# The shared network of the last batch split around the expert loop, in a gated cross-attention and mixture-of-experts block

## The reference

```python
def _L0_xattn_ref(teacher_logits, teacher_features, Wq, bq, Wk, bk):
    query = einsum('bnc,dc->bnd', teacher_features, Wq) + bq
    key = einsum('bnc,dc->bnd', teacher_features, Wk) + bk
    attention = softmax(einsum('bnd,bmd->bnm', query, key), axis=-1)
    return einsum('bln,bmn->blm', teacher_logits, attention)

def _L0_ffn_ref(x, router_w, shared_gate, shared_up, shared_down, w_gate, w_up, w_down):
    flat = x.reshape(-1, 512)
    shared_out = sigmoid(flat @ shared_gate.T) * (flat @ shared_up.T) @ shared_down.T
    weights = softmax(flat @ router_w.T, axis=-1)
    top_w, top_idx = top_k(weights, 2)
    ...
    he = sigmoid(ge) * ue                      # ge, ue, de in bfloat16, for the chosen experts
    routed = (comb[:, :, None] * de).sum(axis=1)
    return x + shared_out + routed

x = x + tanh(g_xattn[0]) * _L0_xattn_ref(_layernorm(x), ctx_1024, ...)
x = x + tanh(g_ffn[0]) * _L0_ffn_ref(_layernorm(x), ...)
```

## Time and profile before

| | us |
|---|---|
| median of three runs (lowest, highest) | 337.62 (336.86, 339.15) |
| span of the profiled execution | 339.6 |
| TensorE busy | 298.9 (88%) |
| VectorE busy | 211.9 (62%) |
| GpSimd busy | 156.9 (46%) |
| ScalarE busy | 136.3 (40%) |
| chain that ended last: PE / DMA / POOL / DVE / issue | 67 / 9 / 6 / 6 / 6% |

### The profile page before, as it was taken

How to read it: one execution, slowest core, us unless ns; L and a number is a source line. 1 busy time by engine, 2 the same in 40 slices (tenths; PEclk the granted TensorE clock), 3 DMA queues, 4 the chain that set the end, 5 groups by cost and what they waited for, 6 DMA issues and landing times.

```text
span 339.6 us, 6123 instructions
## 1 busy us (share of the span) xinstructions
PE 298.9 (88%) x1587; PEld 211.6 (62%) x1599; DVE 211.9 (62%) x580; ACT 136.3 (40%) x239; POOL 156.9 (46%) x237
## 2 busy tenths in 40 slices
PE   2678968999999999999999999699999999998280
PEld 1245845878687786878787787566666666664020
DVE  0147676748874667848357388647767677675191
ACT  1467166740667803657601562033343433333000
POOL 3041978166740384900687117115555656566100
PEclk9959977999999999999999999989999999999587
DMA  4999399512143021000029998224333333429498
GB/s 110 340 294 259 108 198 182 206 49 79 62 130 120 0 80 47 0 2 2 31 94 164 209 207 195 83 74 124 102 120 101 116 97 121 124 79 322 121 312 342
DMA packets 31444, 45.91 MB, mean 135 GB/s; under 512 B 3456, under 2 KB 21120, under 8 KB 31424
## 3 DMA queue, kind: packets, MB, share of 16 engines
q1 hardware_dynamic: 20992, 27.67, 26.7%
q0 software_dynamic: 10432, 17.99, 22.5%
HBM read 39.58 MB, written 14.72 MB: 160 GB/s over the span
## 4 chain that ended last, share of the span: by engine, by line
PE 67%; DMA 9%; POOL 6%; DVE 6%; issue 6%; ACT 2%; SPq 1%; POOLq 0%; ACTq 0%; DVEq 0%
PE bank L675 13%; PE bank L472 11%; PE bank L473 11%; PE bank L474 11%; PE bank L692 7%; POOL xg L398 4%; PE bank L467 4%; DMA acc<-x 4%; PE bank L483 3%; PE bank L667 3%; PE bank L683 2%; DMA z<-ysb,desti 2%; DMA zb<-z 2%; DVE acc L1264 1%; DVE probT_lo L983 1%
## 5 line engine op out<-in xcount | busy, mean ns | idle before, releaser
L888 ACT ACTIVATE sigc<-bank 128x352 f32<-128x352 f32 x39 | 18.1, 463 | 68.1 <-PE bank L675 68.1
L472 PE MATMUL bank<-lnT_hi,sgu_lo 128*128 128x512 f32 (+2 forms) x96 | 39.7, 414 | 1.6 <-DVE lnT_lo L983 1.6
L451 POOL DMA_INDIRECT z<-ysb,desti x36 | 36.1, 1002 | 9.7 <-issue 9.4
L473 PE MATMUL bank<-lnT_lo,sgu_hi 128*128 128x512 f32 (+2 forms) x96 | 38.5, 401 | 0.0
L474 PE MATMUL bank<-lnT_hi,sgu_hi 128*128 128x512 f32 (+2 forms) x96 | 38.4, 400 | 0.0
L675 PE MATMUL bank<-wgu_lo,xTb 128*128 x156 | 36.7, 317 | 0.0
L675 PE MATMUL bank<-wgu_hi,xTb 128*128 x156 | 36.7, 317 | 0.0
L398 POOL DMA_INDIRECT xg<-lnb,slot x32 | 31.9, 996 | 9.9 <-issue 7.3
L1231 DVE TENSOR_TENSOR hrow<-sigc,bank 128x352 bf16<-128x352 f32 x39 | 20.3, 521 | 25.2 <-ACT sigc L888 21.8
L387 POOL TENSOR_TENSOR hT_lo<-sig,hT_hi 128x512 fp32r<-128x512 f32 (+1 forms) x9 | 11.6, 1290 | 47.6 <-ACT hT_hi L798 47.5
L1237 DVE TENSOR_SCALAR ysb<-bank,wt 128x512 bf16<-128x512 f32 x39 | 29.2, 748 | 5.1 <-DMA z<-ysb,desti 2.6
(11 more groups left out here) (174 smaller groups left out, 650.1 us busy)
## 6 DMA issues: line engine op xcount, KB each, us to landing
xt<-xg SPq DMA_DIRECT2D x39, 129.0 KB, 2.1
xT_raw<-xT SPq DMA_DIRECT2D x4, 1024.0 KB, 7.8
acc<-x SPq DMA_DIRECT2D x4, 1024.0 KB, 10.0
out<-acc SPq DMA_DIRECT2D x16, 256.0 KB, 3.4
wgu_lo<-wguT POOLq DMA_DIRECT2D x2, 1408.0 KB, 14.0
wgu_hi<-wguT POOLq DMA_DIRECT2D x2, 1408.0 KB, 13.5
cx<-ctxT SPq DMA_DIRECT2D x4, 512.0 KB, 5.3
wd_sb<-wdT POOLq DMA_DIRECT2D x2, 1024.0 KB, 18.3
```

The lines of the kernel that those rows point to most:

```text
L451: nc.gpsimd.indirect_dma_start(out=z, out_offset=bass.IndirectOffsetOnAxis(ap=desti[:, r:r + 1], axis=0), in_=ysb[:, r, :], in_offset=None ...
L472: pe.matmul(dst, a_lo, b_hi, start=first, stop=False)
L473: pe.matmul(dst, a_hi, b_lo, start=False, stop=False)
L888: act.activation(sigc[:, v, :], bank[2 * v][:, 0:I], ACT.Sigmoid).then_inc(s["csig"], 1)
```

## The change

Three things change, and the order of five engines with them.

1. Of batch 3's shared network only the first piece (c = 0, which holds the logits) is done ahead of the loop; its pieces 1 and 2 and all its `down` rows come behind it. Since the loop uses what lay under them, batch 3's normalised and turned rows go to `probT_hi` and `probT_lo` (`lnT(b)`), and the tiles of the loop and of the tables lie elsewhere.
2. Batch 3's attention is pulled forward: its projections and energies are woven into batch 2's mix, its mix comes ahead of batch 2's pieces 1 and 2, which stand behind it with batch 2's `down` rows last. GpSimd's list is reordered to fit, and `wgu_hi` and `wd_sb` are issued between other pieces of it.
3. The two results of z are no longer added on TensorE. VectorE adds `za` to `acc` for tiles 0 to 5 and `zb` for all 16, GpSimd adds `za` for tiles 6 to 15. `zb` has room for all 16 tiles and comes in eight DMAs.

```diff
+        def gate_bank(b, c):
+            return bank[0 if c == 1 or (b == last_b and c == 0) else 2]
+        def up_bank(b, c):
+            return bank[1 if c == 1 or (b == last_b - 1 and c == 2) else 3]
+        def lnT(b):
+            return (probT_hi, probT_lo) if b == last_b else (lnT_hi, lnT_lo)
...
 @block.sync
-            for t in range(TT):
-                if t >= ZS:
-                    store(t - ZS)
-                sp.dma_start(zb[:, t % ZS], zt[1, :, t]).then_inc(s_zl[t % ZS], 16)
+            for i in range(0, TT, 2):
+                sp.dma_start(zb[:, i:i + 2], zt[1, :, i:i + 2]).then_inc(s_zb[i // 2], 16)
+            for t in range(TT):
+                if t < LT * last_b:
+                    sp.wait_ge(s["comb"], t + 1)
+                else:
+                    sp.wait_ge(s["shared"], t + 1)
+                sp.dma_start(out[t * P:(t + 1) * P, :], acc[:, t, :]).then_inc(s["outd"], 16)
 @block.gpsimd
+            b = last_b - 1
+            factors2(b)
+            factor1(last_b)
+            x_low(last_b)
+            rows_copy(b)
+            pool.wait_ge(s["eng"], TT)
+            pool.wait_ge(s["xTlo"], NB)
+            for k in range(KP, NT):
+                pool.dma_start(wgu_hi[:, k - KP], wguT[:, k * P:(k + 1) * P, :].rearrange("e p i -> p e i")).then_inc(s["wgu2_in"], 16)
+            scatter(b, 0)
+            factors2(last_b)
+            pool.wait_ge(s["xmm"], TT)
+            for k in range(IT):
+                pool.dma_start(wd_sb[0:KI[k], k], wdT[:, k * P:k * P + KI[k], :].rearrange("e p n -> p e n")).then_inc(s["wd_in"], 16)
+            scatter(b, 1)
+            rows_copy(last_b)
+            scatter(last_b, 0)
+            scatter(last_b, 1)
...
+            for t in range(EARLY_Z, TT):
+                pool.wait_ge(s_za[t // LT], 16)
+                nc.gpsimd.tensor_tensor(acc[:, t, :], acc[:, t, :], za[:, t, :], ALU.add).then_inc(s["z1"], 1)
 @block.tensor
+            b = last_b - 1
+            project(last_b, 0)
+            project(last_b, 1)
+            mix(b, range(0, 1))
+            energy(last_b, 0)
+            energy(last_b, 1)
+            mix(b, range(1, 2))
+            energy(last_b, 2)
+            mix(b, range(2, 3))
+            energy(last_b, 3)
+            mix(b, range(3, 4))
+            down(b - 1, 0)
+            turn_prob(last_b, 0)
+            turn_prob(last_b, 1)
+            down(b - 1, 1)
+            turn_ln2(b, 0)
+            turn_ln2(b, 1)
+            down(b - 1, 2)
+            turn_ln2(b, 2)
+            turn_ln2(b, 3)
+            down(b - 1, 3)
+            wide_shared(b, 0, 1)
+            turn_prob(last_b, 2)
+            turn_prob(last_b, 3)
+            wide_shared(b, 0, 0, range(0, 2))
+            turn_logits(b)
+            wide_shared(b, 0, 0, range(2, NT))
+            mix(last_b, range(0, 2))
+            rank(b)
+            mix(last_b, range(2, LT))
+            wide_shared(b, 1, 0)
+            wide_shared(b, 1, 1, range(0, 2))
+            turn_ln2(last_b, 0)
+            turn_ln2(last_b, 1)
+            wide_shared(b, 1, 1, range(2, NT))
+            turn_ln2(last_b, 2)
+            turn_ln2(last_b, 3)
+            wide_shared(b, 2, 0)
+            wide_shared(last_b, 0, 1)
+            wide_shared(b, 2, 1, range(0, 2))
+            turn_logits(last_b)
+            wide_shared(b, 2, 1, range(2, NT))
+            wide_shared(last_b, 0, 0)
+            rank(last_b)
+            for j in range(LT):
+                down(b, j)
...
-            for t in range(TT):
-                pe.wait_ge(s_zl[t % ZS], 16 * (t // ZS + 1))
-                at_least(pe, s["comb"], t - 3)
-                pe.matmul(bank[t % 4][:, :], identb[:], za[:, t, :], start=True, stop=False)
-                pe.matmul(bank[t % 4][:, :], identb[:], zb[:, t % ZS, :], start=False, stop=True).then_inc(s["zsum"], 1)
+            for c in range(1, IT):
+                wide_shared(last_b, c, 0)
+                wide_shared(last_b, c, 1)
+            for parts in (range(IT - 1), range(IT - 1, IT)):
+                for j in range(2):
+                    down(last_b, j, parts)
+            for j in range(2, LT):
+                down(last_b, j)
 @block.vector
+            choose(b)
+            weights(b)
+            residual(last_b, range(0, 2))
+            places(b)
+            shared_hidden(b, 0)
+            hidden_low(b, 0)
+            residual(last_b, range(2, LT))
+            ln2_apply(last_b)
...
+            choose(last_b)
+            shared_hidden(b, 2)
+            hidden_low(b, 2)
+            weights(last_b)
+            places(last_b)
...
+            for t in range(EARLY_Z):
+                add_first(t)
+            shared_hidden(last_b, 1)
+            for r in range(SLOTS):
+                dve.wait_ge(s_yd[r], 16 * len(range(r, NE, SLOTS)))
+            hidden_low(last_b, 1)
+            for t in range(0, 4):
+                add_second(t)
+            shared_hidden(last_b, 2)
+            hidden_low(last_b, 2)
+            for t in range(4, TT):
+                add_second(t)
+            for j in range(LT):
+                shared_out(last_b, j)
```

More of the change, by code:

```diff
@@ L421, in _ @@
                 nc.gpsimd.tensor_copy(lnb_rows[0], lnr2[:]).then_inc(s["rowsb"], 1)
+            for b in range(last_b - 1):
+                factors2(b)
+                if b:
+                    factor1(b + 1)
+                rows_copy(b)
                 if b == 0:
@@ L502, in turn_prob, with mix @@
                 turn(prob[:, j], j).then_inc(s["tp"], 1)
-            def mix(b):
+            def mix(b, rows=range(LT)):
                 pe.wait_ge(s["probTlo"], LT * (b + 1))
                 pe.wait_ge(s["xTlo"], b + 1)
-                for j in range(LT):
+                for j in rows:
                     if j >= 2:
                         pe.wait_ge(s["x1"], LT * b + j - 1)
+                    elif b == last_b:
+                        pe.wait_ge(s["shared"], LT * (b - 2) + j + 3)
                     elif b:
@@ L556, in wide_shared @@
                 else:
-                    pe.wait_ge(s[free], IT * b + 1)
-                o_ = half_ * I + row * P
-                for k in range(NT):
-                    if c == 0 and half_ == 0 and k == NT // 2:
-                        turn_logits(b)
-                    mm = three(bank[pair + half_][0:m, :], sgu_hi[:, k, o_:o_ + m], sgu_lo[:, k, o_:o_ + m],
-                               lnT_hi[:, k, :], lnT_lo[:, k, :], k == 0, k == NT - 1)
-                mm.then_inc(s[done], 1)
+                    pe.wait_ge(s["hid"], IT * b + 1)
@@ L598, in _ @@
             turn_prob(0, 3)
-            for b in range(NB):
-                more = b < last_b
+            for b in range(last_b - 1):
                 mix(b)
@@ L874, in _ @@
                 add_ln2(b, 3)
-                if more:
-                    prob_high(b + 1, 0)
-                    prob_high(b + 1, 1)
+                prob_high(b + 1, 0)
+                prob_high(b + 1, 1)
                 hidden_high(b, 1)
                 gate_shared(b, 2)
-                if more:
-                    prob_high(b + 1, 2)
-                    prob_high(b + 1, 3)
+                prob_high(b + 1, 2)
+                prob_high(b + 1, 3)
                 hidden_high(b, 2)
+            b = last_b - 1
+            qk(last_b)
+            act.activation(warm[:], less_mean[:], ACT.Exp)
+            for j in range(LT):
+                soft(last_b, j)
+            for j in range(LT):
+                normalise(last_b, j)
+            prob_high(last_b, 0)
+            prob_high(last_b, 1)
+            x_high(last_b)
+            for j in range(LT):
+                ln2_high(b, j)
+            rows_again(b)
+            logits_out(b)
+            prob_high(last_b, 2)
+            prob_high(last_b, 3)
+            choice_exp(b)
+            gate_shared(b, 0)
+            for j in range(LT):
+                add_ln2(b, j)
+            hidden_high(b, 0)
+            gate_shared(b, 1)
+            ln2_high(last_b, 0)
+            ln2_high(last_b, 1)
+            hidden_high(b, 1)
+            ln2_high(last_b, 2)
+            ln2_high(last_b, 3)
+            gate_shared(b, 2)
+            rows_again(last_b)
+            logits_out(last_b)
+            act.activation(warm[:], less_mean[:], ACT.Exp)
+            hidden_high(b, 2)
+            choice_exp(last_b)
+            gate_shared(last_b, 0)
+            for j in range(LT):
+                add_ln2(last_b, j)
+            hidden_high(last_b, 0)
             def sigmoid(u, v):
@@ L909, in _ @@
                 step(u // SLOTS, u % SLOTS)
+            for c in range(1, IT):
+                gate_shared(last_b, c)
+                hidden_high(last_b, c)
         @block.vector
@@ L946, in over_sum, with residual @@
                 V.reciprocal(rden[:, j:j + 1], den[:, j:j + 1]).then_inc(s["rden"], 1)
-            def residual(b):
+            def residual(b, rows=range(LT)):
                 dve.wait_ge(s["rstd1"], b + 1)
```

(19 more changed lines are left out.)

326 lines of the change are left out of this document (183 added, 143 removed).

## The result

The changed kernel takes 364.27 us (median of 4 runs, 363.41 to 365.14). The kernel before took 338.38 beside it (4 runs). The ratio is 1.076, with a 95% interval of 1.070 to 1.083: slower, by more than the range of 343 to 361 allowed.

What follows compares the result with a forecast made beforehand. Loop start was taken to go by batch 3's slots + 16.4, not TensorE's work; the tail was added: 339.65 + 6.5 (loop start) + 5.0 (tail) + 0 (GpSimd) + 0.9 (hand-overs) - 2.0 = 350.0 us. Range 345 to 353; 8 in 10, 343 to 361.

Steps and rivals of the forecast that it cites:

- Batch 2's slots: Ahead of the loop: batch 2's routing slots are written at 169.4, where they stood at 160.1.
- the stalls: Batch 2's stage: TensorE's lnr2 transposes wait for VectorE to free banks, about 2.6 us, bounds 0 and twice as much.
- The weights ahead of half a scatter: GpSimd's queue: batch 2's second scatter half waits behind 2.88 MB of wd_sb, landing at about 196 instead of 187.6.
- From the landing to the loop's start: From scatter landing at about 196 through batch 3's row copy, logits and slots (208.8) to loop start at 224.9: +6.5.
- The loop: The expert loop keeps its instructions and its 94.6 us: 0.
- new hand-overs: Across the kernel: some ten new hand-overs between engines, at 0.1 to 0.2 each, add an estimated 0.9 us.
- The tail without contention: Behind the loop: VectorE's 22 additions, where 16 stood, and batch 3's late down rows end at 344.6: +5.0.
- The bank wait and the half clock of the last two down rows: In the tail: third down row waits for VectorE's bank until 334.1; at half clock the rows take 3.9 and 2.3.
- GpSimd's ten additions: In the tail: 12.5 us side by side with VectorE's, costing 0; one at a time, up to +9.
- Rival 1: In the tail: GpSimd's and VectorE's additions exclude each other, +9, giving 359; chance 0.32.
- Rival 3: Ahead of the loop: batch 3's routing follows its mix as before, loop at 210.2 (-8.2), time 332.5; chance 0.07.
- The 2.0 off the sum: Whole kernel: profiled span of 339.65 against the runs' median of 337.6, so 2.0 is taken off at the end.

Runs made afterwards that it cites:

- second profile of before: The kernel before, unchanged, profiled once more: 338.22 us, and 338.36 in the profiled execution, whose span is 336.6.
- e9: Changed kernel with scatter ahead of wd_sb, TensorE summing z for six tiles, last two down rows in free banks: 336.32 us, 0.994 of before.

## Why the prediction was wrong

It had the direction and both mechanisms ahead of the loop, and missed by 14.3 us. By its own steps:

- **Batch 2's slots, +9.3.** They came at 166.0, and at 157.0 in the second profile of before: +9.0. Right, and so are the stalls: in the 47.1 from 117.8 to 164.9 TensorE is busy 44.8, idle 2.3 for the predicted 2.6, most of it ahead of batch 2's transposes, where it waits for VectorE. In absolute time 169.4 had been predicted, 3.4 too late, since the first profiled execution was late by 3.1.
- **The weights ahead of half a scatter.** Right in kind. The wait stood for 12.1 where a DMA of xg ended it, and the exchange of two blocks in one queue removed 14.4. From the weights' first issue to the scatter's landing 18.3 were predicted and 19.9 passed. The Trainium skill (DMA: Bandwidth & Descriptors, "Two DMAs through the same engine are not ordered") says that descriptors within one queue of a DMA engine start in order. The two runs agree: the last landing is 12.7 behind its issue at 181.56 with 2.88 MB ahead of it, and without them the wait is 0.45.
- **From the landing to the loop's start.** 28.9 were predicted and 29.6 passed. TensorE came out of its wait at half clock, and the small products of batch 3's ranks (at 204.4) stand behind eighteen matmuls of 512 columns, fourteen of them at half clock. The loop's start is +8.7 for the predicted +6.5: **this term was 2.2 too small**, 1.6 of it in the DMA queue.
- **The loop.** +0.7 for 0, which is inside the 0.9 that the sum allowed for new hand-overs, so this comes out as 0.2 to the good.
- **The tail without contention, +5.0.** 4.7 with GpSimd's additions left out. The bank wait and the half clock of the last two down rows stand in the trace as described (the third row starts at 351.4 after 6.2 idle, at half clock).
- **GpSimd's ten additions, 0.** **This is the step that failed: it cost 10.9 of the 14.3.** Between two ends, 0 and 9, the sum took 0, on the ground that engines are separate until a row shows otherwise. No row spoke for 0 either: the price of an overlap that no row shows was taken from a row without overlap. The Trainium skill (SBUF — State Buffer, "Who interferes with whom") had said that an instruction of VectorE with two SBUF inputs contends with GpSimd's reads and that the loser blocks, and the runs agree: 12.1 beside GpSimd with both inputs in SBUF, 0.68 with one in PSUM. That the block lasts for a whole run of GpSimd's instructions, ten or four, is what the runs add.
- **Rival 1, 359.** Its exclusion is what happened, and it too was under-priced. It let 3 to 4 of GpSimd's time pass beside VectorE's waits for ScalarE and its reads of PSUM. VectorE works in order, so the blocked addition holds up the harmless instructions behind it, and the whole run of 11.2 counts. GpSimd's addition was 1.15 rather than 1.29. The Trainium skill's GPSIMD Engine Reference ("Elementwise — side-by-side cycle accounting") measures 4497 ns for 2048 columns. A quarter of it, 1.12, is an estimate for 512 columns; the rows here, 1.14 to 1.18, agree within a few per cent.
- **Rival 3's mechanism**, batch 2's scatters landed in time, came out with the exchange: they held up ScalarE's copy by 0.45 only, to 181.8, where the rival had wanted them by 180. The loop starts at 210.1, and 210.2 had been reckoned in the rival; that the two agree is luck, since the baseline was 3 late. As a shift it is -5.1 for -8.2.
- **The 2.0 off the sum** rested on one profiled execution against a median. The spans of all kernels lie 1.8 below their times, so the sum should have been made against 336.6 and 1.8 added: 350.8. This is worth 0.8 of the miss. The changed kernel's median is 0.9 above its own profiled execution.

Together: 10.9 + 2.2 - 0.2 (loop) - 0.3 (tail) + 0.8 + 0.9 = 14.3.

What stays open: why GpSimd keeps VectorE out between two of its instructions. The runs show the length of the block with four and ten instructions, not with gaps between them, and an alternation by semaphores wasn't tried. Why the addition is held that started 0.33 ahead of GpSimd's first is open too. Nor is it shown what made the first 53 us of the first profiled execution 3 longer.

## What to carry to other kernels

Before work is divided between VectorE and GpSimd, list for each VectorE instruction in that stretch how many of its inputs lie in SBUF: here one with two was held for the whole unbroken run of GpSimd's additions, and everything behind it with it. Small transfers on which the next stage waits belong ahead of bulk transfers in the same queue: here two blocks in the other order were worth 14 us. An overlap that no row shows is no reason for a price of nothing.

## What the runs showed of the hardware

- One VectorE addition of 128x512 with both inputs in SBUF lasted 12.1 us beside ten additions of GpSimd of 1.15 each, and 5.4 beside four. The others in the same list took 0.68. In five kernels the held instruction ended 0.55 to 0.56 behind GpSimd's last, and GpSimd's additions took 1.14 to 1.18 each.
- The same addition with its second input in PSUM took 0.68 beside GpSimd's, and a VectorE write to the same tensor was no obstacle. A subtraction of two other SBUF tensors took 7.6 beside them, alone 0.69.
- TensorE was granted half clock after it had stood for 11.1, 7.0 and 6.2 us. Its matmuls of 512 columns were then 0.43 apart (from 197.4, 339.2 and 351.4 on), and 0.23 later.
- The DMAs moved 393 GB/s from 320 to 330 in e9, most of it the output's stores; the stretch in which the casting DMAs of the weights filled the queue had 208.
